# A turn of the context attention with its jobs dealt out anew over four head groups

## The chip, the cores and the metric

The kernel runs on one core of a Trainium2 chip. The metric is the device time of one execution in microseconds (us). The core's engines work side by side, each through its own program in order, and wait for each other on semaphores: PE (TensorE) multiplies and transposes into PSUM, ACT (ScalarE) and DVE (VectorE) drain PSUM and do elementwise work, POOL (GpSimd) works in SBUF, and SP (SyncE) issues loads and stores.

## The reference, cut to what matters

The kernel computes two transformer layers. The change lies in the cross attention of the second one, from 512 rows of each of 8 batches to 77 context rows, with 16 heads of 32 columns:

```python
q = _split_heads(Q @ Wq.T + bq, N_HEAD)
k = _split_heads(K @ Wk.T + bk, N_HEAD)
v = _split_heads(V @ Wv.T + bv, N_HEAD)
score = jnp.einsum('bhqd,bhkd->bhqk', q, k) / jnp.sqrt(jnp.float32(d_k))
attn = jax.nn.softmax(score, axis=-1)
out = jnp.einsum('bhqk,bhkd->bhqd', attn, v)
return out @ Wo.T + bo
...
x = x + jnp.tanh(g_xattn[1]) * _L1_xattn_ref(_layernorm(x, axis=-1), ctx_1024, ctx_1024, ...)
```

Keys and values of the context (k, v) are made long before, in the first pass. What is left here is the normalisation, q, the scores, the softmax, the sum over v, and the projection with Wo.

## The kernel before

The program is a row of passes, with a barrier between two of them. `context_attention_pass` (L1857) is the fifth of seven. It takes a batch of 512 rows in a **turn** `b` (0 to 7), and a turn in four **groups** `c` (0 to 3). Group c does the softmax of four heads at once, the *quad* (b, c). A group has four **slots** j.

Beside this softmax, each turn has sixteen **jobs** for PE. A job fills one of two PSUM banks (`pj_ps`), and another engine drains the bank:

- x0 to x3 (L2090): transposes of the normalised rows (`rows_b`), one of four column blocks each. ACT copies the bank to `xth` rounded (L2169), DVE subtracts to make the rest `xtl` (L2248).
- q0 to q3: products with Wq (`weights_a`), 12 matmuls each, since `split3` (L108) multiplies high and low halves in three terms. ACT drains with the bias (L2175).
- att0 to att3 (L2103): probabilities times values, one for each quad. ACT and DVE drain to `ath` and `atl` (L2178, L2248), as for x.
- out0 to out3: products with Wo (`weights_b`), 12 matmuls each, one for each tile of 128 rows. DVE drains into the residual rows `XR` (L2243).

The jobs are dealt out by hand. `TURN` lists for each group the jobs as (kind, number, lag); lag -1 is a job of the batch before, +1 of the batch after. `SLOT` gives each job its slot. From both comes `SEQUENCE`, the order of all jobs, and from it the bank of each: a job uses the bank of the one two places ahead of it (`former`), and PE waits until that one is drained. `AHEAD` is done before turn 0, `LATE` behind turn 7.

Every engine walks through the same groups and slots (`clock`):

- PE in slot j of group c: the jobs of the slot, then the transposes of head j of the quad before (L2123, into two further banks, "T0" to "T3" below); in slot 1 then also the scores of the next quad (L2114, "S1" in group 0 to "S0" of the next batch in group 3). The scores have one buffer and wait until DVE has subtracted in it.
- DVE: at a group's start the maximum (L2254) and the subtraction (L2257) of the quad's scores, then the drains of slots 0 and 1, then the sums (L2264) and their reciprocal (L2266), then the drains of slots 2 and 3. In slot 3 of group 1 come the statistics of the rows of batch b + 2 (L574 to L584), in slot 3 of group 3 their scaling (L589). In the last two turns there are none; in group 1 of both stands the split of a weight of the next pass (L2282).
- ACT: the exponential (L2198) at slot 1, ahead of the drains of that slot; each head's transposes are copied (L2183), and att needs all four copies of its quad.
- POOL: probabilities times reciprocals (L2063), which T0 waits for; the bias onto the residual rows (L2055) in group 0.
- SP: keys of the next batch behind S1 and S3, values behind att3, the store of a batch and the reload of `XR` behind its out3.

```python
earlier = former(turn, task)
if earlier:
    pe.wait_ge(taken[earlier[0]], earlier[2] * C + earlier[1] + 1)
```

These lines of `job` on PE (L2084 and after) are the wait for the bank.

## Time and profile before

| | us |
|---|---|
| median of 3 runs | 2549.83 |
| lowest and highest | 2549.44, 2553.63 |
| the profiled execution | 2550.44 |
| its span | 2548.7 |
| PE busy | 2326.8 |
| DVE busy | 1390.9 |
| ACT busy | 1060.3 |
| POOL busy | 607.2 |
| context attention, from the first transposes to the last product | 1489.2 to 1884.9 |

A row of the timeline gives the start and the length of an instruction or of a run of equal ones, and in brackets how long its engine was idle before it and who released it. Matmuls overlap: the distance from one start to the next start tells how long PE was kept. A product is twelve rows of L108 at 0.23 us from start to start. The granted clock of TensorE is 1.00 at 2.4 GHz and 0.50 at 1.2 GHz.

### The profile page before, as it was taken

How to read it: one execution, taken by the hardware profiler on the slowest of the kernel's cores; microseconds unless marked ns; L12 is line 12 of the kernel's file. 1: busy time of each engine (PE TensorE's matmuls, PEld its weight loads, DVE VectorE, ACT ScalarE, POOL GpSimd, SP SyncE). 2: the span in 40 equal slices, each digit the busy share in tenths (PEclk: the TensorE clock that was granted, in tenths of full speed). 3: DMA queues.
4: the chain of work that ended last, by engine and by line, in shares of the span. 5: the costliest groups of instructions: out<-in, count | busy, mean ns of one | idle time of the engine just before them, and what ended most of it. 6: DMA issues, size and time to landing. Idle time of an engine off the chain costs nothing. (4 is left out here: it accounts for less than half of the span.)

```text
span 2548.7 us, 40730 instructions
## 1 busy us (share of the span) xinstructions
PE 2326.8 (91%) x16307; PEld 1545.2 (61%) x16348; DVE 1390.9 (55%) x1717; ACT 1060.3 (42%) x1228; POOL 607.2 (24%) x213
## 2 busy tenths in 40 slices
PE   8899999999999987899999779999878999999989
PEld 6655554555555544455555346766656888888867
DVE  7665646556555444777777567677534222222235
ACT  5445445454454442555555544444433222211223
POOL 0045546455464651000000013323210000000000
PEclk9899999999999988999999989999988999999989
DMA  9410101101010103111111221222231000000046
GB/s 299 183 40 12 50 10 48 43 11 47 10 49 11 42 30 113 45 51 50 55 56 34 69 79 58 73 81 77 93 115 55 33 33 33 33 18 32 17 165 215
DMA packets 102014, 163.73 MB, mean 64 GB/s; under 512 B 16996, under 2 KB 39524, under 8 KB 99102
## 3 DMA queue, kind: packets, MB, share of 16 engines
q1 hardware_dynamic: 95918, 150.82, 17.9%
q10 hardware_dynamic: 6000, 11.54, 1.2%
q8 instruction: 71, 1.16, 0.2%
q14 instruction: 25, 0.20, 0.0%
HBM read 112.63 MB, written 49.71 MB: 64 GB/s over the span
## 5 line engine op out<-in xcount | busy, mean ns | idle before, releaser
L1152 DVE TENSOR_REDUCE att_mx<-att_sn 128x2 f32<-128x1024 f32 x196 | 239.8, 1223 | 150.8 <-PE att_sn L961 148.9
L1061 ACT ACTIVATE att_num<-att_st 128x2048 f32<-128x2048 f32 x128 | 240.5, 1879 | 148.2 <-PE att_st L942 89.6
L865 POOL TENSOR_TENSOR att_es<-att_es,att_num 128x2048 f32<-128x2048 f32 x64 | 294.6, 4604 | 15.0 <-ACT att_num L1061 8.7
L861 POOL TENSOR_TENSOR att_es<-att_num 128x2048 f32<-128x2048 f32 x32 | 145.8, 4557 | 366.0 <-PE att_pj L922 341.6
L2541 ACT ACTIVATE rec_ga<-rec_g,rec_bg 128x512 f32<-128x512 f32 x84 | 57.1, 687 | 309.2 <-PE rec_g L2442 309.2
L2442 PE MATMUL rec_g<-weights_a_h,row_weights_h 128*128 128x512 f32 x384 | 153.6, 400 | 14.0 <-ACT rec_ga L2541 11.1
L2442 PE MATMUL rec_g<-weights_a_l,row_weights_h 128*128 128x512 f32 x384 | 152.1, 396 | 0.0
L2442 PE MATMUL rec_g<-weights_a_h,row_weights_l 128*128 128x512 f32 x384 | 151.8, 395 | 0.0
L562 POOL TENSOR_TENSOR ffn_ln_rstd<-ffn_ln_var,ffn_ln_power 128x4 f32<-128x4 f32 x8 | 22.0, 2755 | 464.0 <-DVE ffn_ln_var L584 464.0
L1475 PE MATMUL ffn_h<-ffn_xqt,ffn_w 128*128 128x512 bf16 x486 | 116.3, 382 | 16.3 <-DVE ffn_hs L1736 12.8
L2063 POOL TENSOR_TENSOR xat_pr<-xat_e,xat_rd 128x1232 f32<-128x1232 f32 x32 | 72.9, 2278 | 244.2 <-DVE xat_rd L2266 237.5
L915 PE MATMUL att_pj<-att_num,att_v 128*32 128x512 f32 x1024 | 125.1, 608 | 0.9 <-DVE att_rd L1134 0.9
L1736 DVE TENSOR_TENSOR ffn_hs<-ffn_h,ffn_fb 128x1024 f32<-128x1024 f32 x64 | 78.1, 1220 | 83.1 <-PE ffn_h L1475 83.1
L1488 PE MATMUL ffn_c<-ffn_hs,ffn_dg 32*32 32x512 f32 x3072 | 110.5, 606 | 8.2 <-issue 5.3
L2606 DVE SCALAR_TENSOR_TENSOR rec_ga<-rec_ga,rec_c 128x512 f32<-128x512 f32 x32 | 22.1, 691 | 172.7 <-ACT rec_ga L2541 172.7
L562 POOL TENSOR_TENSOR rec_ln_rstd<-rec_ln_var,rec_ln_power 128x4 f32<-128x4 f32 x7 | 7.5, 1067 | 421.4 <-DVE rec_ln_var L584 421.4
L1624 ACT ACTIVATE ffn_ss<-ffn_c,conv_bias 128x512 f32<-128x512 f32 x128 | 77.4, 692 | 67.2 <-PE ffn_c L1488 61.5
L961 PE MATMUL att_sn<-att_kh,att_qh 32*128 32x512 f32 x392 | 96.5, 487 | 8.9 <-DVE att_mx L1152 8.7
L2183 ACT ACTIVATE xat_pt<-xat_pt 77x512 f32<-77x512 f32 x128 | 73.6, 588 | 74.6 <-PE xat_pt L2123 74.2
L961 PEld LDWEIGHTS att_sn<-att_kh,att_qh 32*128 32x128 f32 x392 | 37.3, 185 | 107.8 <-DVE att_mx L1152 57.0
L1475 PEld LDWEIGHTS ffn_h<-ffn_xqt,ffn_w 128*128 128x128 bf16 x512 | 46.9, 99 | 84.3 <-DVE ffn_hs L1736 19.3
L2123 PEld LDWEIGHTS xat_pt<-xat_ident,xat_pr 128*77 128x77 f32 x512 | 64.9, 157 | 50.1 <-issue 20.8
(407 smaller groups left out, 5800.6 us busy)
## 6 DMA issues: line engine op xcount, KB each, us to landing
rows<-in_x SPq DMA_DIRECT2D x16, 1024.0 KB, 5.4
rows<-x SPq DMA_DIRECT2D x16, 1024.0 KB, 5.2
rows_b<-in_fside_BxSxS SPq DMA_DIRECT2D x8, 1024.0 KB, 7.9
heads<-att_o SPq DMA_DIRECT2D x32, 256.0 KB, 2.3
weights_b_l<-heads SPq DMA_DIRECT2D x8, 1024.0 KB, 5.3
x<-ffn_xr SPq DMA_DIRECT2D x32, 256.0 KB, 2.1
xat_xr<-x SPq DMA_DIRECT2D x8, 1024.0 KB, 5.2
out_x<-x SPq DMA_DIRECT2D x8, 1024.0 KB, 8.8
```

What stands on the lines that cost most here:

```text
L861: pool.tensor_tensor(ES[:], E[0][:], E[1][:], ALU.add).then_inc(s_sum, 1)
L865: pool.tensor_tensor(ES[:], ES[:], E[k][:], ALU.add).then_inc(s_sum, 1)
L915: last = pe.matmul(out[heads(j), :], V[:, k, c * P + DH * j:c * P + DH * j + DH], E[k][:, j, :], start=(k == 0), stop=(k == T - 1))
L961: last = pe.matmul(sn_ps[:, r, :], QT[0][c][own, m // 2 * P:m // 2 * P + P], KT[0][c][own, :], start=True, stop=True)
L1061: act.activation(E[k][:], st_ps[:], ACT.Exp, scale=SCALE).then_inc(s_exp, 1)
L1152: dve.tensor_reduce(MX[c % 2][:, m // 2, 2 * DH * (m % 2):2 * DH * (m % 2) + DH + 1:DH], sn_ps[:], AX, ALU.max, negate=True).then_inc(s_ma ...
L1475: last = pe.matmul(h_ps[:, m, :], W1[:, k, i * P:i * P + P], XQT[:, k, :], start=(k == 0), stop=(k == C - 1))
L1488: last = pe.matmul(c_ps[quarter(m), r, :], DG[quarter(r), 3 * (HG * group + m) + k, :], HS[group % 2][quarter(r), m, k:k + S], start=(k == ...
L1624: act.activation(SS[:, i, :], c_ps[:, r, :], ACT.Silu, bias=CB[:, i:i + 1]).then_inc(s_silu, 1)
L1736: dve.tensor_tensor(HS[group % 2][:, 2 * half:2 * half + 2, 1:S + 1], h_ps[:], FB[:].unsqueeze(1).broadcast_to([P, 2, S]), ALU.mult).then_ ...
L2183: act.activation(PT[d % 2][j][:], pt_ps[j % 2][0:G, :], ACT.Copy).then_inc(s_pte, 1)
L2442: last = pe.matmul(g_ps[m % 2][n][:], W[n][a][:, k, m * P:m * P + P], R[c][:, k, :], start=(part == 0 and k == 0 and i == 0), stop=((part ...
```

## The change

The two tables and the list of jobs ahead of turn 0 are changed, nothing else:

```diff
-    TURN = [[("att", 2, -1), ("q", 3, 0), ("x", 0, 1), ("x", 1, 1), ("x", 2, 1), ("x", 3, 1)],
-            [("att", 3, -1), ("q", 0, 1), ("out", 0, -1), ("out", 1, -1)],
-            [("out", 2, -1), ("out", 3, -1), ("att", 0, 0)],
-            [("att", 1, 0), ("q", 1, 1), ("q", 2, 1)]]
-    SLOT = {("att", 2): 0, ("q", 3): 1, ("x", 0): 2, ("x", 1): 2, ("x", 2): 3, ("x", 3): 3,
-            ("att", 3): 0, ("q", 0): 1, ("out", 0): 2, ("out", 1): 3,
-            ("out", 2): 0, ("out", 3): 1, ("att", 0): 2,
-            ("att", 1): 0, ("q", 1): 1, ("q", 2): 2}
-    AHEAD = [("x", c, 0) for c in range(C)] + [("q", c, 0) for c in range(3)]
+    TURN = [[("q", 2, 0), ("att", 2, -1), ("q", 3, 0)],
+            [("att", 3, -1), ("x", 0, 1), ("x", 1, 1), ("out", 0, -1), ("out", 1, -1)],
+            [("out", 2, -1), ("x", 2, 1), ("x", 3, 1), ("out", 3, -1), ("att", 0, 0)],
+            [("q", 0, 1), ("att", 1, 0), ("q", 1, 1)]]
+    SLOT = {("q", 2): 0, ("att", 2): 1, ("q", 3): 2,
+            ("att", 3): 0, ("x", 0): 1, ("x", 1): 1, ("out", 0): 2, ("out", 1): 3,
+            ("out", 2): 0, ("x", 2): 1, ("x", 3): 1, ("out", 3): 2, ("att", 0): 3,
+            ("q", 0): 0, ("att", 1): 1, ("q", 1): 2}
+    AHEAD = [("x", c, 0) for c in range(C)] + [("q", c, 0) for c in range(2)]
```

On PE a turn reads, before and after, with the transposes of heads (T) and scores (S) in their places:

| group | before | after |
|---|---|---|
| 0 | att2 T0 q3 T1 S1 x0 x1 T2 x2 x3 T3 | q2 T0 att2 T1 S1 q3 T2 T3 |
| 1 | att3 T0 q0 T1 S2 out0 T2 out1 T3 | att3 T0 x0 x1 T1 S2 out0 T2 out1 T3 |
| 2 | out2 T0 out3 T1 S3 att0 T2 T3 | out2 T0 x2 x3 T1 S3 out3 T2 att0 T3 |
| 3 | att1 T0 q1 T1 S0 q2 T2 T3 | q0 T0 att1 T1 S0 q1 T2 T3 |

The first place is the step from group 1 to group 2 on DVE, in the loop over the middle turns. `rows` and `xat_ln` belong to the statistics, `xat_mx` and `xat_sm` to the scores, `xat_xr` is the drain of out, `xat_xtl` that of x. Before:

```order
L580 MEMSET xat_ln_var 128x4
L582 BN_AGGR xat_ln_mv<-xat_ln_stats 128x2 x4
L52 REGISTER_ALU
L584 TENSOR_REDUCE xat_ln_var<-xat_ln_mv 128x4
L2253 REGISTER_ALU
L2254 TENSOR_REDUCE xat_mx<-xat_s 128x16
L2257 TENSOR_TENSOR xat_sm<-xat_s,xat_mx 128x1232
L2243 SCALAR_TENSOR_TENSOR xat_xr<-xat_pj,xat_tg,xat_xr 128x512 x2
L2264 TENSOR_REDUCE xat_su<-xat_e 128x16
```

The same place after:

```order
L580 MEMSET xat_ln_var 128x4
L582 BN_AGGR xat_ln_mv<-xat_ln_stats 128x2 x4
L52 REGISTER_ALU
L584 TENSOR_REDUCE xat_ln_var<-xat_ln_mv 128x4
L2253 REGISTER_ALU
L2254 TENSOR_REDUCE xat_mx<-xat_s 128x16
L2257 TENSOR_TENSOR xat_sm<-xat_s,xat_mx 128x1232
L2243 SCALAR_TENSOR_TENSOR xat_xr<-xat_pj,xat_tg,xat_xr 128x512
L2247 REGISTER_ALU
L2248 TENSOR_TENSOR xat_xtl<-xat_pj,xat_xth 128x512
```

Out2's drain is where it was, behind the statistics, the maximum and the subtraction; out3's has moved behind the drains of x2 and x3 and the sums.

The second place is group 2 on PE in turn 6, written out without the loop. There the last matmuls of out2 were followed by T0 and out3:

```order
L108 MATMUL xat_pj<-weights_b_h,xat_atl 128x512
L2123 MATMUL xat_pt<-xat_ident,xat_pr 77x128 x4
L108 MATMUL xat_pj<-weights_b_h,xat_ath 128x512
L108 MATMUL xat_pj<-weights_b_l,xat_ath 128x512
L108 MATMUL xat_pj<-weights_b_h,xat_atl 128x512
```

After the change:

```order
L108 MATMUL xat_pj<-weights_b_h,xat_atl 128x512
L2123 MATMUL xat_pt<-xat_ident,xat_pr 77x128 x4
L2090 MATMUL xat_pj<-xat_ident,rows_b 128x128 x8
L2123 MATMUL xat_pt<-xat_ident,xat_pr 77x128 x4
L2114 MATMUL xat_s<-xat_k,xat_qt 128x77 x16
L108 MATMUL xat_pj<-weights_b_h,xat_ath 128x512
```

The transposes x2 and x3 (L2090, eight matmuls), a transpose of heads and the scores S3 stand between out2 and out3.

## Rows read from the trace of the kernel before

**Rows 1.** The page's first part: busy time of the engines.

```profile
PE 2326.8 (91%) x16307; PEld 1545.2 (61%) x16348; DVE 1390.9 (55%) x1717; ACT 1060.3 (42%) x1228; POOL 607.2 (24%) x213
```

**Rows 2.** Windows: start:end, length, busy time per engine, PEclk, DMA share, GB/s.

```profile
1489.20:1549.20 60.00, 49.99 (x348) 36.45 (x348) 38.91 (x56) 23.29 (x35) 12.68 (x8) 0.77 0.27 81
1549.20:1816.90 267.70, 246.15 (x2021) 186.53 (x2017) 188.34 (x237) 126.10 (x194) 86.74 (x35) 1.00 0.25 82
1816.90:1885.80 68.90, 54.31 (x328) 38.52 (x324) 36.89 (x46) 22.30 (x33) 18.93 (x7) 0.80 0.18 60
```

**Rows 3.** Timeline of PE, a middle turn: start, length, instruction, [idle before <- releaser].

```profile
1642.92 1.09 PE L2090 MATMUL xat_pj<-xat_ident,rows_b 128*128 128x128 f32 x8
1643.85 0.60 PE L2123 MATMUL xat_pt<-xat_ident,xat_pr 128*77 128x128 f32 x4
1644.99 1.25 PE L2090 MATMUL xat_pj<-xat_ident,rows_b 128*128 128x128 f32 x8 [0.54 <-DVE xat_xtl L2248]
1647.45 1.06 PE L2103 MATMUL xat_pj<-xat_pt,xat_v 77*32 77x512 f32 x8 [0.78 <-DVE xat_xtl L2248]
...
1659.44 0.60 PE L2123 MATMUL xat_pt<-xat_ident,xat_pr 128*77 128x128 f32 x4
1659.79 0.48 PE L108 MATMUL xat_pj<-weights_b_h,xat_ath 128*128 128x512 f32 x1
...
1662.67 0.60 PE L2123 MATMUL xat_pt<-xat_ident,xat_pr 128*77 128x128 f32 x4
...
1670.31 1.06 PE L2103 MATMUL xat_pj<-xat_pt,xat_v 77*32 77x512 f32 x8 [0.73 <-ACT xat_pt L2183]
1671.80 0.66 PE L2123 MATMUL xat_pt<-xat_ident,xat_pr 128*77 128x128 f32 x4 [0.42 <-POOL xat_pr L2063]
...
1681.49 1.06 PE L2103 MATMUL xat_pj<-xat_pt,xat_v 77*32 77x512 f32 x8 [0.95 <-ACT xat_pt L2183]
...
1686.28 1.13 PE L2114 MATMUL xat_s<-xat_k,xat_qt 32*128 32x77 f32 x32
1687.34 1.09 PE L2090 MATMUL xat_pj<-xat_ident,rows_b 128*128 128x128 f32 x8
```

**Rows 4.** Timeline of DVE in the same turn.

```profile
1659.63 0.75 DVE L2243 SCALAR_TENSOR_TENSOR xat_xr<-xat_pj,xat_tg,xat_xr 128x512 f32<-128x512 f32 x1 [2.49 <-PE xat_pj L108]
1660.30 2.46 DVE L574 BATCH_NORM_STATS2 xat_ln_stats<-rows 128x6 f32<-128x512 f32 x4
...
1663.32 1.44 DVE L2254 TENSOR_REDUCE xat_mx<-xat_s 128x16 f32<-128x1232 f32 x1
...
1666.15 1.40 DVE L2243 SCALAR_TENSOR_TENSOR xat_xr<-xat_pj,xat_tg,xat_xr 128x512 f32<-128x512 f32 x2
...
1675.91 3.85 DVE L589 TENSOR_SCALAR rows_b<-rows,xat_ln_mv,xat_ln_rstd 128x512 f32<-128x512 f32 x4
```

**Rows 5.** Timeline of PE: three of its idle stretches over 2 us.

```profile
88.39 1.97 PE L885 MATMUL att_st<-ident,rows 128*128 128x128 f32 x8 [3.71 <-ACTq L1012]
...
1822.90 1.13 PE L2114 MATMUL xat_s<-xat_k,xat_qt 32*128 32x77 f32 x32 [2.14 <-DVE xat_sm L2257]
...
2436.67 0.77 PE L108 MATMUL rec_pj<-row_weights_h,rec_ch 128*128 128x512 f32 x1 [7.17 <-DVE row_weights_l L2375]
```

**Rows 6.** Windows of two falls of the clock, behind waits of 2.67 and 2.14 us.

```profile
899.40:902.80 3.40, 3.40 (x26) 1.53 (x18) 1.38 (x2) 0.60 (x1) 0.00 (x0) 0.50 0.00 0
1824.40:1834.60 10.20, 9.06 (x60) 5.91 (x58) 6.45 (x7) 4.54 (x8) 7.75 (x3) 0.50 0.39 119
```

**Rows 7.** Timeline of PE at half clock: scores, a product, the transposes behind it.

```profile
1830.78 2.01 PE L2114 MATMUL xat_s<-xat_k,xat_qt 32*128 32x77 f32 x32
1832.71 0.79 PE L108 MATMUL xat_pj<-weights_b_h,xat_ath 128*128 128x512 f32 x1
...
1836.48 0.60 PE L2123 MATMUL xat_pt<-xat_ident,xat_pr 128*77 128x128 f32 x4
```

**Rows 8.** Timeline of PE, turn 7: the scores behind out3.

```profile
1848.05 1.13 PE L2114 MATMUL xat_s<-xat_k,xat_qt 32*128 32x77 f32 x32 [1.27 <-DVE xat_sm L2257]
```

## The prediction, written before the changed kernel had run

> **What bounds the kernel now.** TensorE is busy for 91% of the span [rows 1], so I look first for the places where it stands idle inside the edited pass, and then for what it would wait on in the new order. The pass takes 396.6 us. Its middle, turns 1 to 6, is 267.7 us long and TensorE works in 246.2 us of it at a granted clock of 1.00 (2.4 GHz); the start and the end of the pass have lower shares and a lower mean clock, 0.77 and 0.80 [rows 2]. The middle repeats itself exactly: the first two transposes of rows start at 1642.92 us and again at 1687.34 us, so a turn is 44.42 us [rows 3]. In it PE stands idle five times, for 0.54 us (x2 waits until VectorE has drained x0), 0.78 (att3 waits for x1's drain), 0.73 (att1 waits for the copies of its transposes), 0.42 (the transposes wait for POOL's probabilities) and 0.95 us (att2 waits for copies) [rows 3]. That is 3.42 us in a turn. More than that times seven, 24 us or 0.9% of the kernel, no new order can win in this pass.
>
> VectorE is the other engine to watch. It is in order: what stands behind the moments in its program waits for them. In [rows 4] it drains out1 at 1659.63, takes the four statistics from 1660.30, then the maximum and the subtraction of group 2 from 1663.32 on, and only then drains out2, from 1666.15 on. Now this costs PE nothing: behind out2 come out3, two transposes and the scores, and nothing asks for out2's bank before att0.
>
> **The change, part by part.** No instruction is added or taken away: 16 jobs in a turn, each with the same shape. What changes is what stands between two jobs of the same bank, since a job waits until the job two places ahead of it is drained.
>
> *Waits that go.* Now there are two products in every group. x2 and x3 no longer follow x0 and x1 directly: 0.54 and some 0.18 us inside the second pair go. att3 no longer follows x3: 0.78 goes. att1 now has q0 and a transpose ahead of it, so its copies and POOL's probabilities are in time: 0.73 and 0.42 go. The 0.95 us stay: "product, two transposes, att" is still there, now ahead of att3 in place of att2. Together 2.65 us less in a turn.
>
> *The wait that comes: x3 on out2's drain.* The new sequence is out0, out1, out2, x2, x3, out3. x3 uses out2's bank and comes after one product, one transpose and x2. Counted from the transposes behind out1 (1659.44 in the old trace): 0.35 to out2, 2.88 for it, 0.60 for transposes that no product follows, 0.47 for x2 make 4.30 us until PE wants x3 [rows 3]. VectorE's work between out1 and out2 is the same as before (the order above): out2's drain starts 6.71 us after those transposes (1666.15), takes 0.75, and PE starts some 0.15 later: 7.6 us [rows 4]. So x3 waits 7.6 - 4.30 = **3.3 us** in each of turns 1 to 5. In turn 6, as in turn 7, a weight split stands in place of the moments, and the subtraction ends later: S3, which PE would want 7.1 us behind those transposes (two products of 2.88, three transposes of 0.35, 0.35 and 0.60), waits 1.27 us for it there [rows 8]; with the drain of 0.75 that makes 7.1 + 1.27 + 0.75 - 4.30, some 4.8 us. Everything behind x3 on PE (transposes, S3, out3, att0) is held up with it, and POOL and ScalarE only follow.
>
> *Smaller waits that come.* S1 is now in group 0, after two products, but group 0's maximum and subtraction come behind the scaling of the rows (3.85 us [rows 4]), and the chain to them starts at att0, which has moved a slot later. Between nothing and the 2.14 us that S1 waits for the same subtraction in the last turn [rows 5]; I take 0.6, nearer to nothing, since two products, five transposes and att2 (some 8.7 us) lie between S0 and S1, and the scaling, the maximum and the subtraction behind it come to about 7, only starting late. x1 now waits for att3's drain and out0 for x0's: each between 0 and the 0.78 us of the wait of this kind in [rows 3]; I take 0.4 and 0.2. With 0.2 for two transposes fewer that a product follows, a steady turn gets 3.3 + 0.6 + 0.4 + 0.2 + 0.2 - 2.65 = **2.05 us longer**.
>
> *Sum without the clock.* Turns 1 to 6: 6 x 2.05 = 12.3, and 1.5 more for turn 6. Turn 0 has no out products to hide behind; q2 now comes later and fills one of its waits: between 0 and -4, I take -2. In turn 7 out3 no longer stands ahead of S3, which waits for VectorE anyway (1.27 us [rows 8]), but behind it and ahead of att0, from which the closing chain runs: out3 and its transposes, 3.2 us, and 0.8 for a longer wait of S1: +4. That makes **+16 us**.
>
> *The clock.* This is the larger unknown. I listed all idle stretches of PE of over 2 us that began at full clock: 14 in the whole trace; the first ends at 88.39, the shortest, of 2.14 us, at 1822.90, the last at 2436.67 [rows 5]. After every one of them the granted clock was 0.50 (1.2 GHz) for a stretch, of 3.4 us the shortest, 10.2 us for the one behind the 2.14 us [rows 6]. In turns 1 to 6 there is no such wait so far, and the clock is 1.00 throughout. A wait of 3.3 us is of this kind, so I expect a fall in each of turns 1 to 6. What is then slower: scores take 1.93 us in place of 1.06, and a product in whose course the clock comes back 3.77 in place of 2.88 [rows 3, 7]; with x3 and a transpose (1.0 us, doubled) that is 0.87 + 0.89 + 0.97 = **2.7 us** for one fall, 16 us for six. Bounds: 0, and 5.1 us (10.2 us at half clock, PE working all through).
>
> The Trainium skill, "TensorE: Matmul & The Clock Gate", section "HAM oscillation — how this bites in real kernels", puts the penalty at half of the throttled time, paid anew at every long gap of a loop. By this page and the 10.2 us of [rows 6] it would be 31 us for six falls and the sum +47. This trace has falls of 3.4 us too [rows 6], and for those the same rule gives 1.7 us each.
>
> Sum: 16 + 16 = **+32 us**. The profiled execution took 2550.44 us, of which 2548.7 are the span; the median of the three runs is 2549.83, 0.6 us less. I go from the median: 2582 us.
>
> **Nothing else.** The loads are not nearer to their use: keys, values and the reload of the residual rows follow S1, att3, S3 and the last out, and the residual rows are needed some 10 us after they land. The passes behind this one start after a barrier and only shift.
>
> **The rivals.**
> 1. *Forecast*: new wait of x3, and the clock falls behind it. +32, own range +24 to +40. For it: 14 of 14. Chance 0.67; falls in some turns only lie between this and the next, in the range of either.
> 2. *The wait comes, the clock stays up.* PE has worked densely until x3, and short transposes surround the wait; its length could spare it. +16: 2566. Chance 0.15.
> 3. *Long falls.* A fall lasts 10.2 us every time, PE working in all of it: 6 x 5.1 = 31, +47: 2597. For it: the fall behind the shortest of the 14 waits was that long; against it: others last 3.4 us, and out3 and q0 are dense work [rows 6]. Chance 0.08. It is the price that the page named above gives.
> 4. *No change.* x3 waits 1.3 us only, because the statistics are finished ahead of out1's end, and the gains of 2.65 cancel the small waits. Against it: they stand behind out1's drain in VectorE's program. 0.03.
> 5. *Faster.* The mechanism is the one the even split suggests: out2's drain comes early enough, x3 doesn't wait. Then a turn gets 3.3 - 2.05 = 1.25 us shorter, 7.5 us over six, 2 in turn 0, less 4 in turn 7: -5.5, 2544. It decides at a wait of 3.3 - 2.05 = 1.25 us for x3: below it a turn is shorter, above it longer. This needs VectorE to drain out2 some 2 us sooner than [rows 4] shows, with the same instructions ahead. Chance 0.07, with errors in my reading of the order.
>
> **How the numbers follow.** A measurement of this kernel can tell 0.2%, 5 us. Predicted is the forecast, 2582. The range of 2564 to 2592 holds the forecast's own and rival 2; left out are rivals 3 to 5, 0.18. Slower 0.90 (the first three), same 0.03, faster 0.07.
>
> **What would show it.** In the table of waits a new line, PE x transposes waiting for VectorE's drain of the output (L2090 on L2243), six times, some 21 us; the lines for PE waiting for the row drains (xtl) and for POOL shrink in the middle of the pass. A turn of 48 to 50 us in place of 44.4, or 46.5 if the clock holds. In the windows of the turns a granted clock under 1.00. Wrong would be: a turn under 44.4; no such line; or falls of the clock without a longer turn. VectorE's, ScalarE's and POOL's busy times stay as they are; PE's grows by what runs at half clock.

## The result and the profile after

The changed kernel takes 2573.39 us (median of 4 runs, 2570.99 to 2577.69) against 2550.05 us (4 runs, 2549.44 to 2553.63): the ratio is 1.0093, with an interval of 1.0077 to 1.0109. It is 23.3 us slower. The forecast was 2582 us, the range 2564 to 2592. The profiled execution took 2574.59 us, 2572.8 of which are the span.

The page's busy times after the change, which answer to [rows 1]:

```profile
PE 2340.6 (91%) x16348; PEld 1554.2 (60%) x16348; DVE 1390.9 (54%) x1717; ACT 1055.8 (41%) x1228; POOL 607.4 (24%) x213
```

VectorE's and POOL's times are the same within 0.2 us, ScalarE's is 4.5 us shorter, for which no cause was looked for. PE is busy for 13.8 us more, though it has the same work. 5.3 us of them lie ahead of the pass, where nothing was changed (1347.2 and 1352.4 us) and where the trace of before lacks the 41 matmul records by which 16307 and 16348 differ. Inside the pass it is 11.5 us more, since some of the work now runs at a lower clock, and behind it 2.9 less.

Windows of the kernel after, for the start, the middle and the end of the pass, cut like [rows 2] at T0 of group 0 in turns 1 and 7 (start:end, length, busy us and instructions of PE, PEld, DVE, ACT and POOL, granted clock, DMA share, GB/s):

```profile
1489.80:1546.90 57.10, 47.72 (x341) 36.95 (x342) 36.33 (x55) 21.94 (x34) 12.80 (x8) 0.78 0.25 69
1546.90:1837.10 290.20, 259.44 (x2018) 196.24 (x2016) 190.21 (x239) 122.96 (x194) 86.74 (x35) 0.95 0.24 79
1837.10:1912.40 75.30, 54.81 (x333) 40.08 (x331) 36.22 (x45) 22.15 (x34) 18.93 (x7) 0.82 0.16 55
```

The pass, from its first transposes to its last product, grew from 395.7 to 422.7 us, by 27.0. The middle accounts for most of it: 267.7 us at a granted clock of 1.00 became 290.2 us at 0.95, +22.5. The start is 2.9 us shorter. The end is 7.3 us longer (its last product ended at 1884.9 before, and ends at 1912.4 now). Of both, 1.0 us is only where the cut stands: att2 comes ahead of T0 before and behind it after, so for the same work the start is 1.9 us shorter and the end 6.3 us longer. Outside the pass the program is 0.6 us longer ahead of it and 3.4 us shorter behind it (660.4 us against 663.8). Together that is +24.1 in the span.

The new line in the table of waits after the change (engine and line, released by; us in total, times, the longest), with the two that grew, for the whole pass:

```profile
PE xat_pj L2090 <- DVE xat_xr L2243: 20.9, 6, 4.6
PE xat_s L2114 <- DVE xat_sm L2257: 9.6, 10, 4.1
PE xat_pt L2123 <- POOL xat_pr L2063: 9.5, 3, 3.3
```

The first line is the wait that the prediction named, six times and 20.9 us. The scores waited 6.5 us, 5 times, in the pass before, and the transposes of heads 8.1 us, 10 times, for POOL; these 10 are now 3, two in the first turn and one in the last.

PE's timeline of the kernel after, in a middle turn, answers to [rows 3] (start, length, instruction, [idle before <- releaser]):

```profile
1654.45 0.66 PE L2090 MATMUL xat_pj<-xat_ident,rows_b 128*128 128x128 f32 x4 [0.40 <-DVE xat_atl L2248]
...
1665.98 0.60 PE L2123 MATMUL xat_pt<-xat_ident,xat_pr 128*77 128x128 f32 x4
1666.42 0.60 PE L2090 MATMUL xat_pj<-xat_ident,rows_b 128*128 128x128 f32 x4
1670.26 0.66 PE L2090 MATMUL xat_pj<-xat_ident,rows_b 128*128 128x128 f32 x4 [3.25 <-DVE xat_xr L2243]
1670.76 0.60 PE L2123 MATMUL xat_pt<-xat_ident,xat_pr 128*77 128x128 f32 x4
1671.29 1.49 PE L2114 MATMUL xat_s<-xat_k,xat_qt 32*128 32x77 f32 x32
1672.71 0.79 PE L108 MATMUL xat_pj<-weights_b_h,xat_ath 128*128 128x512 f32 x1
...
1676.78 0.60 PE L2123 MATMUL xat_pt<-xat_ident,xat_pr 128*77 128x128 f32 x4
```

x2 (1666.42) has its bank, x3 (1670.26) has not, and idles for 3.25 us. VectorE's timeline of the kernel after shows why; it answers to [rows 4]:

```profile
1662.95 0.75 DVE L2243 SCALAR_TENSOR_TENSOR xat_xr<-xat_pj,xat_tg,xat_xr 128x512 f32<-128x512 f32 x1 [2.48 <-PE xat_pj L108]
1663.62 2.46 DVE L574 BATCH_NORM_STATS2 xat_ln_stats<-rows 128x6 f32<-128x512 f32 x4
...
1666.63 1.44 DVE L2254 TENSOR_REDUCE xat_mx<-xat_s 128x16 f32<-128x1232 f32 x1
1668.11 1.44 DVE L2257 TENSOR_TENSOR xat_sm<-xat_s,xat_mx 128x1232 f32<-128x1232 f32 x1
1669.47 0.74 DVE L2243 SCALAR_TENSOR_TENSOR xat_xr<-xat_pj,xat_tg,xat_xr 128x512 f32<-128x512 f32 x1
```

The drain of out1 starts at 1662.95 and the drain of out2 at 1669.47, 6.52 us apart, as in [rows 4] (1659.63 and 1666.15). The order on VectorE and its durations are the old ones. What changed is only that PE now asks for out2's bank early.

Behind the wait the clock falls. A window of the kernel after, 1.6 us behind x3's start:

```profile
1671.90:1675.30 3.40, 3.40 (x26) 2.78 (x23) 2.32 (x4) 0.36 (x1) 0.88 (x1) 0.50 0.12 23
```

There is one such fall with each of the six waits, 3.4 us long in turns 2 to 5 and 6.8 us in turns 1 and 6. In turn 1 it begins 0.8 us before the wait ends, in the others behind it. From x3 to the next transposes of heads (1670.26 to 1676.78) PE needs 6.52 us. At full clock the same four pieces (0.50 for x3, 0.53 for a transpose, 1.06 for the scores, 2.88 for a product) make 4.97. So a fall of 3.4 us costs 1.55 us here. A turn is 47.67 us long (the rows' first transposes start at 1653.44 and again at 1701.11); it was 44.42.

### The profile page after: what moved, and what is told of

Its sections match the earlier page's. It is cut to its first block and busy times, and to the rows that moved or that the text cites. A ratio compares the mean times of both kernels' runs of the same rounds, so it can differ in the third digit from the quotient of the medians.

```text
span 2572.8 us, 40766 instructions
## 1 busy us (share of the span) xinstructions
PE 2340.6 (91%) x16348; PEld 1554.2 (60%) x16348; DVE 1390.9 (54%) x1717; ACT 1055.8 (41%) x1228; POOL 607.4 (24%) x213
## 5 line engine op out<-in xcount | busy, mean ns | idle before, releaser
L1475 PE MATMUL ffn_h<-ffn_xqt,ffn_w 128*128 128x512 bf16 x512 | 123.8, 385 | 12.8 <-DVE ffn_hs L1736 12.8
L1475 PEld LDWEIGHTS ffn_h<-ffn_xqt,ffn_w 128*128 128x128 bf16 x512 | 47.2, 99 | 85.4 <-issue 20.9
```

The lines of the kernel that those rows point to most:

```text
L1475: last = pe.matmul(h_ps[:, m, :], W1[:, k, i * P:i * P + P], XQT[:, k, :], start=(k == 0), stop=(k == C - 1))
```

## The experiments

Every kernel was timed beside the kernel before on the same chip. "Before" in a ratio is that one, with medians of 2548.1 to 2549.0 us. A kernel derived from "the changed kernel" keeps its tables except where the diff says otherwise.

### 1. The changed kernel, its statistics taken elsewhere

The statistics of group 1 (3.0 us of VectorE's work with what is computed from them, 1663.62 to 1666.63 above) move one slot earlier, from behind out1's drain to ahead of it. PE's program is left as it is.

```diff
-                    if not last and j == 3 and c in (1, 3):
-                        normalise(b + 2, c // 2)
+                    if not last and (c, j) in ((1, 2), (3, 3)):
+                        normalise(b + 2, ((1, 2), (3, 3)).index((c, j)))
```

> The changed kernel with the row statistics of VectorE moved one slot earlier in group 1: from behind the drain of out1 to between the drains of out0 and out1, so that they run beside PE's product out1. Theory A (x3 waits 3.25 us because statistics, maximum and subtraction stand between the drains of out1 and out2): 3.06 us leave that stretch, x3's wait falls to under 0.6 us, the turn from 47.7 to about 44.2 us, no fall of the clock in turns 1 to 5, and the whole to about 2552 us (2546 to 2557), turn 6 keeping its long wait since a weight split stands there. Theory B (VectorE has simply too much to do in group 1, 11 us of work): the wait only moves, to out0's or out1's bank or to S3, and the whole stays at 2568 or more.

Measured: 2550.16 us (10 runs), ratio 1.0001, interval 0.9992 to 1.0011. VectorE's timeline of this kernel has the statistics between out0's and out1's drains now, and only the maximum and the subtraction between those of out1 (1606.44) and out2 (1609.93):

```profile
1603.42 2.46 DVE L574 BATCH_NORM_STATS2 xat_ln_stats<-rows 128x6 f32<-128x512 f32 x4
...
1606.44 0.75 DVE L2243 SCALAR_TENSOR_TENSOR xat_xr<-xat_pj,xat_tg,xat_xr 128x512 f32<-128x512 f32 x1
1607.11 1.43 DVE L2254 TENSOR_REDUCE xat_mx<-xat_s 128x16 f32<-128x1232 f32 x1
1608.57 1.44 DVE L2257 TENSOR_TENSOR xat_sm<-xat_s,xat_mx 128x1232 f32<-128x1232 f32 x1
1609.93 0.74 DVE L2243 SCALAR_TENSOR_TENSOR xat_xr<-xat_pj,xat_tg,xat_xr 128x512 f32<-128x512 f32 x1
```

PE's timeline has the wait of x3 at 0.66 us:

```profile
1610.72 0.66 PE L2090 MATMUL xat_pj<-xat_ident,rows_b 128*128 128x128 f32 x4 [0.66 <-DVE xat_xr L2243]
```

The line of waits of this kernel, for the pass:

```profile
PE xat_pj L2090 <- DVE xat_xr L2243: 7.9, 6, 4.6
```

A turn takes 43.57 us and the clock doesn't fall in turns 1 to 5. Of the six waits five are short; turn 6 keeps its 4.63 us and its fall, since there the weight split stands in that place and not the statistics. This is the decisive run: with PE's order untouched, moving 3 us of another engine's work removes the whole slowdown (1.0093 to 1.0001). With the statistics there a middle turn is 0.85 us shorter than in the kernel before (0.37 us shorter than in experiment 4, where the old tables have the statistics in the same place). This is lost again in turn 6, which is some 5 us longer than before, and at the end of the pass, where the waits of 3.12, 4.06 and 6.07 us described below remain.

### 2. The wait filled with work, the clock held

Ahead of x3 PE makes 26 transposes into a bank that is free there. Nobody reads them; the wait stays, only PE isn't idle in it.

```diff
+                if kind == "x" and i == 3 and not (isinstance(turn, int) and turn == -1):
+                    pe.wait_ge(s_pte, turn * H + HG)
+                    for _ in range(26):
+                        pe.transpose(pt_ps[1][:, 0:P], ident[:], ident[:])
```

> The changed kernel with 26 transposes of the identity into a free bank ahead of x3's wait (some 3.0 us of PE work that nobody reads), so that the wait stays as long but PE is not idle in it. If the falls of the clock behind that wait cost what the trace says (1.5 us where they last 3.4 us, 2.8 us in turn 1), the turns 2 to 5 go from 47.66 to 46.1 us, and the whole is 8 to 12 us shorter, near 2563. Theory of no cost (PE would catch up elsewhere in the turn, since S1 waits for VectorE anyway): the same 2573 within 3 us. If idle alone, not its depth, decided, the clock would still fall.

Measured: 2564.53 us (4 runs), ratio 1.0055, interval 1.0039 to 1.0072. PE's timeline of this kernel, where the wait was, and two windows: five of its turns, and its whole middle, cut as above:

```profile
1661.72 3.00 PE L2088 MATMUL xat_pt<-xat_ident 128*128 128x128 f32 x26
1665.13 0.66 PE L2094 MATMUL xat_pj<-xat_ident,rows_b 128*128 128x128 f32 x4 [0.41 <-DVE xat_xr L2247]
```

```profile
1556.00:1786.70 230.70, 220.54 (x1813) 169.90 (x1812) 162.43 (x210) 99.42 (x161) 73.53 (x31) 1.00 0.22 72
1545.97:1824.34 278.37, 264.60 (x2174) 203.83 (x2172) 190.08 (x239) 122.85 (x194) 86.81 (x35) 1.00 0.25 82
```

x3 starts as late as ever, but the clock is 1.00 over five whole turns, and a turn takes 46.15 us. By the ratios (1.0093 against 1.0055) the clock's part of the slowdown is 0.0038 of 2550 us, about 9.7 us; by the medians it is 8.9. What is left, 14 to 16 us, is the wait itself and the longer end. A turn of the loop shows the split: 44.42 without the wait, 46.15 with it, 47.67 with a fall of 3.4 us, so 1.73 for the order of work and 1.52 for the clock, near the 1.55 us read from the timeline. Counted from T0 of group 0 to the next, turn 1 is 49.03 us against 46.32, turns 2 to 5 are 1.50 to 1.54 us apart, and turn 6 is 50.51 against 47.45. So the six falls cost 2.7, four times 1.5, and 3.1 us: 11.8 us, which is also the difference of the two middles (290.2 and 278.4). In the total 8.9 of them arrive. The two traces differ by 1 to 2.5 us each at the start of the pass, ahead of it and behind it too.

### 3. x2 and x3 behind out3

The two transposes of rows get one more product's time before they ask for their banks.

```diff
-            [("out", 2, -1), ("x", 2, 1), ("x", 3, 1), ("out", 3, -1), ("att", 0, 0)],
+            [("out", 2, -1), ("out", 3, -1), ("x", 2, 1), ("x", 3, 1), ("att", 0, 0)],
```

> The changed kernel with x2 and x3 behind out3 (slot 2 of group 2) in place of ahead of it. Theory A: out3 is then the cover for out2's drain, and x3 waits for out3's drain instead, which VectorE does behind the sums; S3 stands ahead of out3 and waits for the subtraction some 2.7 us. So the wait moves from x3 to S3 and the turn stays within 0.5 us of what it is (47.2 to 47.7 us), the whole at 2568 to 2574. If only the place of x3 mattered: the turn falls by 3 us or more, the whole to 2553 or less.

Measured: 2574.44 us (4 runs), ratio 1.0092, interval 1.0075 to 1.0109: the same as the changed kernel. It is 0.4 us over the expected range. x3 waits 0.48 us, and this line of waits has grown (it was 9.6 us):

```profile
PE xat_s L2113 <- DVE xat_sm L2256: 30.9, 16, 4.1
```

The scores S3 now wait 2.68 us in each of turns 1 to 5 for the subtraction of group 2, which stands behind the same statistics, and behind each of these waits the clock falls for 3.4 us too. In turn 6, behind the weight split, they wait 4.06 us and the fall lasts 6.8 us. A turn is 47.63 us. PE must not want anything of VectorE's between out1's drain and out2's earlier than VectorE gets there; which of PE's steps asks is unimportant.

### 4. The kernel before, its statistics moved in the same way

The statistics' new place without the new tables: the diff is that of experiment 1, on the kernel before.

> The kernel before with the same move of the statistics, from slot 3 to slot 2 of group 1. It tells how much of a1's gain belongs to the statistics in any order. Nothing waits for VectorE behind out1 there, except in the last two turns; replayed with the trace's durations, POOL's probabilities of group 2 come earlier, and the turn falls by 0.6 us: 2546 us (2543 to 2550), a gain of 0.1 to 0.2%. If the gain is as large as a1's (over 10 us), theory A's reading, that the new order created the stretch, is wrong.

Measured: 2547.61 us (10 runs), ratio 0.9994, interval 0.9984 to 1.0004. A turn takes 43.94 us in place of 44.42. In the old order the move takes 0.48 us off a turn, too little for the total to show clear of noise; in the new one it is worth 24 us. So experiment 1 didn't find a general gain of that size that happens to cancel a loss. With the statistics in this place both tables are alike: 1.0001 and 0.9994, their intervals overlapping.

### 5. The queries' move alone

The half of the change that touches q and out: x0 to x3 stay in group 0. (The diffs here and in experiment 6 are against the kernel before. Here and in experiments 3, 6 and 10 the slots and the jobs ahead of turn 0 follow the table; the diff shows the table alone.)

```diff
-    TURN = [[("att", 2, -1), ("q", 3, 0), ("x", 0, 1), ("x", 1, 1), ("x", 2, 1), ("x", 3, 1)],
-            [("att", 3, -1), ("q", 0, 1), ("out", 0, -1), ("out", 1, -1)],
+    TURN = [[("q", 2, 0), ("att", 2, -1), ("q", 3, 0), ("x", 0, 1), ("x", 1, 1), ("x", 2, 1), ("x", 3, 1)],
+            [("att", 3, -1), ("out", 0, -1), ("out", 1, -1)],
...
-            [("att", 1, 0), ("q", 1, 1), ("q", 2, 1)]]
+            [("q", 0, 1), ("att", 1, 0), ("q", 1, 1)]]
```

> One part of the change alone: the products are dealt out as in the changed kernel (q2, q3 in group 0, q0, q1 in group 3, two products in every group), the four transposes of rows stay together in group 0 as before. Theory A: x3 no longer waits for out2. But group 1 then holds no q between att3 and out0, so PE comes to out1 and S3 sooner and VectorE's statistics, maximum and subtraction end last all the same: S3, in slot 1 of group 2 with only out2 ahead of it, waits some 2.7 us, S2 some 1 us, a turn takes 47 us without falls of the clock, and the whole 2570 to 2580, as slow as the full change. Rival: the rows' transposes are what costs, and without their move the even deal of products pays: a turn under 44.4 us and the whole under 2550.

Measured: 2583.96 us (4 runs), ratio 1.0144, interval 1.0127 to 1.0161: 4 us over what was expected. The waits came as expected (S3 2.68 us, S2 1.02 us), but not the clock: it falls in every one of turns 1 to 6. PE's timeline and the table of waits of this kernel:

```profile
1625.59 2.00 PE L2113 MATMUL xat_s<-xat_k,xat_qt 32*128 32x77 f32 x32 [2.68 <-DVE xat_sm L2256]
```

```profile
PE xat_s L2113 <- DVE xat_sm L2256: 39.4, 23, 4.1
```

With q0 gone from group 1, S3 comes too early for the subtraction of group 2, as in experiment 3. The turns alternate between some 48.5 and 50 us, as the falls behind the waits do between 3.4 and 6.8 us. This half of the change is worse than the whole: in the changed kernel x0 to x3 stand in the time that q0's leaving opens ahead of S3, and S3 doesn't wait there in turns 1 to 6.

### 6. The rows' transposes alone

The other half: x0 and x1 in group 1, x2 and x3 in group 2; q2 stays in group 3.

```diff
-    TURN = [[("att", 2, -1), ("q", 3, 0), ("x", 0, 1), ("x", 1, 1), ("x", 2, 1), ("x", 3, 1)],
-            [("att", 3, -1), ("q", 0, 1), ("out", 0, -1), ("out", 1, -1)],
-            [("out", 2, -1), ("out", 3, -1), ("att", 0, 0)],
-            [("att", 1, 0), ("q", 1, 1), ("q", 2, 1)]]
+    TURN = [[("att", 2, -1), ("q", 3, 0)],
+            [("att", 3, -1), ("x", 0, 1), ("x", 1, 1), ("out", 0, -1), ("out", 1, -1)],
+            [("out", 2, -1), ("x", 2, 1), ("x", 3, 1), ("out", 3, -1), ("att", 0, 0)],
+            [("q", 0, 1), ("att", 1, 0), ("q", 1, 1), ("q", 2, 1)]]
```

> The other part alone: rows' transposes two and two behind att3 and out2, out3 behind S3 and q0 in group 3 as in the changed kernel, q2 still ahead of the batch's turn (three products in group 3, one in group 0). Theory A: the stretch from out1 to x3 is the same, x3 waits 3.25 us for out2's drain, the clock falls behind it, a turn takes some 48 us, the whole 2570 to 2580. Rival: the wait needs q2's move too: a turn under 46 us.

Measured: 2587.46 us (4 runs), ratio 1.0156, interval 1.0139 to 1.0173: 7 us over what was expected. PE's timeline, the table of waits and a window behind one of the waits:

```profile
1672.49 0.66 PE L2089 MATMUL xat_pj<-xat_ident,rows_b 128*128 128x128 f32 x4 [3.25 <-DVE xat_xr L2242]
```

```profile
PE xat_pj L2089 <- DVE xat_xr L2242: 20.9, 6, 4.6
```

```profile
1673.60:1680.40 6.80, 6.80 (x44) 5.60 (x45) 2.84 (x4) 0.89 (x2) 3.23 (x2) 0.50 0.06 12
```

The wait is that of the changed kernel to the hundredth, in each turn and in total. The pass is 434.3 us long, 11.7 more than in the changed kernel. From turn 1's rows to turn 7's it is 6.8 us (1558.04 to 1804.25, against 1556.92 to 1796.37). Its falls in turns 1 to 6 last 6.8, 3.4, 6.8, 6.8, 6.8 and 10.2 us, where the changed kernel has 6.8, 3.4 four times and 6.8; the one turn with a fall of 3.4 us is the shortest, 48.10 us against 49.30 to 49.66. What goes with the length is when the fall begins: in both kernels those that begin 1.4 us or more behind x3's start last 3.4 us, and those that begin earlier, from 2.1 us ahead of that start to 1.1 us behind it, last 6.8 or 10.2. Why the moment differs from kernel to kernel and from turn to turn wasn't settled.

### 7. A table made for VectorE's order

If the reason is that PE asks VectorE for something too early, then a table whose jobs ask late enough should beat both kernels. Of PE's jobs and VectorE's instructions with the durations and waits of these traces I worked out a table in which the jobs of a middle turn should hardly wait; its statistics stand in slot 1 of group 2.

```diff
+    TURN = [[("q", 1, 0), ("att", 2, -1), ("q", 2, 0), ("q", 3, 0)],
+            [("x", 0, 1), ("att", 3, -1), ("x", 1, 1), ("x", 2, 1), ("out", 0, -1), ("x", 3, 1)],
+            [("out", 1, -1), ("out", 2, -1), ("q", 0, 1)],
+            [("out", 3, -1), ("att", 0, 0), ("att", 1, 0)]]
+    SLOT = {("q", 1): 0, ("att", 2): 0, ("q", 2): 1, ("q", 3): 3, ("x", 0): 0, ("att", 3): 1,
+            ("x", 1): 1, ("x", 2): 3, ("out", 0): 3, ("x", 3): 3, ("out", 1): 0, ("out", 2): 1,
+            ("q", 0): 3, ("out", 3): 0, ("att", 0): 0, ("att", 1): 2}
+    AHEAD = [("x", c, 0) for c in range(C)] + [("q", c, 0) for c in range(1)]
...
+                    if not last and (c, j) in ((2, 1), (3, 3)):
+                        normalise(b + 2, ((2, 1), (3, 3)).index((c, j)))
```

> A table of its own, found by replaying the waits with the trace's durations: q1, q2, q3 in group 0, the rows' transposes singly between other jobs (x0, x1, x2, x3 in slots 0, 1, 3, 3 of group 1, each with a job of another kind between), out0 to out3 from the end of group 1 on, q0 at the end of group 2, att0 and att1 in group 3, and the statistics in slot 1 of group 2, behind the drain of out2. Every drain then has a product or several jobs to hide behind. Expected: a turn of 40.8 us, no idle of PE over 1 us in it and no fall of the clock, the pass 40 us shorter than before, the whole at 2508 us (2500 to 2518). If VectorE's chain through the softmax and not the order of the drains bounded the turn, it would stay over 43 us and the whole over 2535.

Measured: 2515.21 us (4 runs), ratio 0.9869, interval 0.9852 to 0.9885. One turn and all of the middle of this kernel, as windows:

```profile
1627.70:1668.50 40.80, 40.63 (x338) 30.84 (x337) 31.93 (x43) 19.93 (x33) 14.45 (x7) 1.00 0.26 85
1545.00:1790.00 245.00, 242.76 (x2012) 184.16 (x2011) 188.23 (x239) 123.20 (x194) 84.85 (x35) 1.00 0.27 89
```

A turn is 40.83 us, and PE is busy in 40.63 of the 40.80 us shown; the same 16 jobs took 44.42 and 47.67. The total lies in the expected range. The pass is 360.0 us long, 35.7 less than before, where 40 were expected. By PE's busy time hardly anything is left in the middle for another order. The prediction's bound was 3.42 us in a turn, its waits; 44.42 - 40.83 is 3.59, all of it and 0.17 more.

### 8. Experiment 1 with the weights' split two groups later

If turn 6's 4.63 us come from the weight split in its group 1, they go when the split does. All three splits of the next pass's weights come two groups later, on ScalarE and VectorE:

```diff
-                at = (b - B + 2) * C + c if isinstance(b, int) else -1
+                at = (b - B + 2) * C + c - 2 if isinstance(b, int) else -1
```

> a1 (statistics in slot 2) with the three splits of the next pass's weights in the last two turns two groups later, so that turn 6 has none in group 1. Theory A holds for the end as for the middle: turn 6's wait of x3 (4.63 us) is the split standing between the drains of out1 and out2, so it goes to under 1.5 us, and the whole is 4 to 9 us shorter than a1 (2550.2), near 2543. If that wait came from something else in turn 6, nothing changes.

Measured: 2548.13 us (10 runs), ratio 1.0000, interval 0.9990 to 1.0009. PE's timeline of this kernel at x3 in turn 6:

```profile
1787.07 0.66 PE L2090 MATMUL xat_pj<-xat_ident,rows_b 128*128 128x128 f32 x4 [0.29 <-DVE xat_xr L2243]
```

The wait is gone as expected (0.29 for 4.63), and the pass is 390.9 us, 6.1 less than in experiment 1: the middle is 7.3 us shorter and the end 1.1 us longer, where a split now stands (the last product waits 4.78 us for VectorE in place of 3.06). But the profiled spans are alike (2546.9 and 2547.0 us), and so are the ratios. The pass begins 2.5 us later in this trace, and the part behind it is 3.4 us longer (663.8 and 660.4 us). There, with the same instructions, the clock is at 0.50 for 34.8 us in this trace and for 27.2 in experiment 1's. This expectation wasn't borne out for the total: a gain of 6 us inside the pass didn't arrive at the end of the program.

### 9. Experiment 7 with the statistics at their old place

Which part of experiment 7's gain is the table's and which the statistics' is told by leaving them at the end of group 1:

```diff
-                    if not last and (c, j) in ((2, 1), (3, 3)):
-                        normalise(b + 2, ((2, 1), (3, 3)).index((c, j)))
+                    if not last and j == 3 and c in (1, 3):
+                        normalise(b + 2, c // 2)
```

> best1's table of jobs with the statistics where they were, in slot 3 of group 1. It tells the table's share of best1's gain from the statistics' share. In this table out0 is drained ahead of x3 in that slot and the statistics stand behind both; out1 comes in group 2. By theory A the statistics then delay only the maximum and subtraction of group 2 and out1's drain, which out2, T1 and S3 cover: a turn of 41.1 us (best1: 40.83), the whole at 2517 us, 0 to 7 us more than best1. If the statistics' place were what made best1 fast, it would be over 2530.

Measured: 2520.06 us (4 runs), ratio 0.9880, interval 0.9861 to 0.9899. A turn is 41.11 us, as expected. By the ratios the statistics' new place is worth 0.0011, 3 us, with intervals that overlap: a table whose jobs don't ask between out1's and out2's drains hardly minds where the statistics are. The table is the gain.

### 10. A second table, with the late split

Another table of the same kind, with statistics in the last slot of group 2 and the split of experiment 8, to see how much depends on the one table.

```diff
+    TURN = [[("q", 1, 0), ("att", 2, -1), ("q", 2, 0), ("q", 3, 0)],
+            [("x", 0, 1), ("att", 3, -1), ("x", 1, 1)],
+            [("out", 0, -1), ("out", 1, -1), ("x", 2, 1), ("x", 3, 1), ("out", 2, -1), ("q", 0, 1)],
+            [("out", 3, -1), ("att", 0, 0), ("att", 1, 0)]]
```

> A second table found in the same way, with out0 and out1 both in slot 0 of group 2, x2 and x3 behind them, statistics in slot 3 of group 2, and the weight splits two groups later. By replay a turn of 40.7 us and an end some 3 us shorter than best1's: 2511 us (2505 to 2518), that is no measurable difference or a small gain over best1's 2515. PE is then busy for all but 0.5 us of a turn, so a turn well under 40.6 us would speak against the reading that PE bounds it.

Measured: 2514.53 us (4 runs), ratio 0.9858, interval 0.9838 to 0.9878: not to be told from experiment 7. A turn is 40.67 us, as expected; the shorter end isn't there (the pass is 361.6 us, 1.6 more than in experiment 7). One turn of this kernel as a window:

```profile
1587.90:1628.50 40.60, 40.53 (x338) 30.87 (x336) 32.03 (x43) 19.55 (x33) 14.46 (x7) 1.00 0.25 85
```

## Why the prediction was right, and where it was not

The total, 2573.39 us, lies in the range, which was drawn around rivals 1 and 2 together. Measured from the median it started from, +23.6, it is just short of the forecast's own +24 to +40: mechanism and places came as said, the sum was a good third too high.

**The wait that comes** was right in place, cause and size: forecast 3.3 us in turns 1 to 5 and some 4.8 in turn 6, measured 3.25 and 4.63, 20.9 us in all against "some 21". Experiment 1 shows the cause: take the statistics out from between the two drains, and the wait is 0.66.

**That the clock falls behind it** was right (six waits, six falls), and experiment 2 shows that it falls because PE idles. **Its price** is the term that was mis-sized: 2.7 us for one fall and 16 us for six were forecast. The falls of 3.4 us cost 1.5 each, those of 6.8 us 2.7 and 3.1, all six 11.8 (experiment 2). The 2.7 us were worked out for a fall that begins together with x3. In turns 2 to 5 it begins 1.5 to 1.9 us behind x3's start, at 1671.9 in the rows above. I had let x3 and the transpose behind it run at half clock too (0.97); from 1670.26 to 1671.29 they take 1.03 us, as at full clock. The scores I had wholly at half clock (0.87 more); to the product's start they take 1.42 in place of 1.06, 0.36 more. The product, for which [rows 7] gave 0.89 more, took 1.19 (4.07 for 2.88, 1672.71 to 1676.78). 0.36 + 1.19 is the 1.55: the step that failed is the one that let every fall begin together with x3. The rule of the Trainium skill ("TensorE: Matmul & The Clock Gate", section "HAM oscillation — how this bites in real kernels"), half of the throttled time, gives 1.7 us for a fall of 3.4 us and 3.4 for one of 6.8. The traces, 1.5 and 2.7 to 3.1, lie somewhat below both. The price of the long falls (10.2 us each, rival 3) didn't come: none of the six was longer than 6.8 us.

**The small terms of a turn.** S1 waits 0.23 us where 0.6 was taken; x1 0.40, as taken; out0 some 0.1 where 0.2 was taken. The turn without the clock was forecast at 44.42 + 2.05 = 46.47 us and is 46.15 in experiment 2. The 1.5 us more for turn 6 were counted wrongly. The forecast added x3's longer wait, but turn 6 of the kernel before already waits for the same weight split, at S3, and that wait goes. PE's timeline of the kernel before, turn 6:

```profile
1800.98 1.13 PE L2114 MATMUL xat_s<-xat_k,xat_qt 32*128 32x77 f32 x32 [1.27 <-DVE xat_sm L2257]
```

So turn 6 without the clock is 1.8 us longer (45.61 to 47.45), where 2.05 + 1.5 = 3.55 were forecast. Turns 1 to 6 together: forecast 12.3 + 1.5 + 16, some +30; measured +22.5, of which 10.7 are the order and 11.8 the clock.

**The start** gave 1.9 us on the same work where I took 2 from between 0 and 4. That is luck in part: the q2 term was an estimate without rows, and the clock is low there in both traces (0.77 and 0.78), so what is the order and what the clock wasn't told apart. **The end** was forecast at +4 and is +6.3 on the same work. PE's timeline of the kernel after, turn 7 and what follows; the fence answers to [rows 5] and [rows 8]:

```profile
1842.41 1.90 PE L2114 MATMUL xat_s<-xat_k,xat_qt 32*128 32x77 f32 x32 [3.12 <-DVE xat_sm L2257]
...
1868.97 1.22 PE L2114 MATMUL xat_s<-xat_k,xat_qt 32*128 32x77 f32 x32 [4.06 <-DVE xat_sm L2257]
...
1885.53 1.14 PE L2123 MATMUL xat_pt<-xat_ident,xat_pr 128*77 128x128 f32 x4 [6.07 <-ACT xat_pt L2183]
1889.73 3.81 PE L2123 MATMUL xat_pt<-xat_ident,xat_pr 128*77 128x128 f32 x16 [3.06 <-POOL xat_pr L2063]
...
1898.49 0.77 PE L108 MATMUL xat_pj<-weights_b_h,xat_ath 128*128 128x512 f32 x1 [2.98 <-DVE xat_atl L2248]
```

The last three of these in the kernel before:

```profile
1859.17 1.14 PE L2123 MATMUL xat_pt<-xat_ident,xat_pr 128*77 128x128 f32 x4 [3.86 <-ACT xat_pt L2183]
1862.77 3.81 PE L2123 MATMUL xat_pt<-xat_ident,xat_pr 128*77 128x128 f32 x16 [2.46 <-POOL xat_pr L2063]
...
1871.68 0.77 PE L108 MATMUL xat_pj<-weights_b_h,xat_ath 128*128 128x512 f32 x1 [1.53 <-DVE xat_atl L2248]
```

S1 waits 3.12 in place of 2.14, 1.0 more where I had 0.8. S3 waits 4.06 in place of 1.27: out3 is no longer ahead of it, which I had said, and had priced as out3 and its transposes (3.2 us) behind it. What I left out are the waits that come after, in the closing chain: 6.07 in place of 3.86, 3.06 in place of 2.46 and 2.98 in place of 1.53 us. That they grew because less of PE's work is left to stand in them is the likely reason, not one that a run shows.

**Behind the pass** I had written "only shift". It became 3.4 us shorter, with the same instructions: the clock is at 0.50 there for 27.1 us, and was for 34.8 before. That lies outside anything I had a term for. Summed, on the same work: start -1.9, middle +22.5, end +6.3, ahead +0.6, behind -3.4 make +24.1 in the span; the medians differ by 23.3. The forecast of +32 was 8.7 too high against these 23.3. The middle makes +7.5 of that (30 for 22.5; some 4.4 of them are the clock, 1.7 turn 6, the rest the small terms), the part behind the pass +3.4 and the difference of medians and spans +0.8; the end makes -2.3, the part ahead -0.6 and the start -0.1. So errors of both signs stand in the sum.

**The bound** of 24 us, which "no new order can win in this pass", was wrong. It was worked out from the waits of a middle turn, and the tables of experiments 7 and 10 made the pass 35.7 and 34.1 us shorter. 21.6 us of experiment 7's gain lie in the middle. The other 14 lie in the start and the end, where PE was idle for 10 and some 14 us by [rows 2], which the bound had left out. The forecast doesn't rest on it.

**The signs.** The new line of waits came, six times and 20.9 us. The turn came out at 47.67 us, just under the "48 to 50" that was written down, for the reason given for the price.

**The rivals.** Rival 2 (the clock stays up, +16) isn't what happened, but it is what experiment 2 made, at 1.0055, +14. Rival 4 (statistics finished ahead of out1's end) fell: the statistics start at 1663.62, behind out1's drain. Rival 5 (no wait of x3, -5.5) names the point that decides, x3's wait of 1.25 us. Experiment 1 lies below it, at 0.66, and its turn is indeed shorter, 43.57 (also than the 43.94 of experiment 4, so that this isn't the statistics' place alone). Its total isn't faster, because of turn 6 and the end. Those two terms would have to be taken away too, and in experiment 8 one of them was, with no gain in the total.

**What stays open.** How the time outside the pass answers to a shift of a few us (experiment 8); and what sets the moment at which a fall begins, with which its length goes (experiment 6).

## What to carry to other kernels

Before moving jobs of one engine, write down what the other engine does in order between two drains of the same ring of buffers, and count from the last common event when the mover will ask and when the drain can come: here that gave 3.3 us for 3.25. If a gap can't be closed by the mover's order, look at the other engine's order too: in the changed kernel, moving 3 us of its work that nobody waits for just then was worth 24 us, and a table that heeds its order is 33 to 34 us faster than the kernel before. An even split of work over groups says nothing about when it is asked for; and where TensorE's wait can't be avoided, filling it can keep the clock up, which was worth 9 us here, a good third of the damage.

## What the runs showed of the hardware

- Idles of PE of 2.1 us and more were mostly followed by a fall of the granted clock from 1.00 to 0.50 (2.4 to 1.2 GHz): 14 of 14 in the kernel before, and every wait of 2.68 us in experiment 3. In the traces of all twelve kernels it was 200 of 211 (of those that began at full clock, without the one ahead of the first matmul). The eleven others, from 2.20 to 3.72 us long, lie in nine kernels. One is in experiment 2: PE's timeline of that kernel, and the windows of the idle and of what follows it:

```profile
1515.74 0.66 PE L2127 MATMUL xat_pt<-xat_ident,xat_pr 128*77 128x128 f32 x4 [3.14 <-POOL xat_pr L2063]
```

```profile
1512.50:1515.80 3.30, 0.16 (x2) 0.06 (x1) 3.23 (x4) 0.69 (x1) 2.25 (x1) 1.00 0.00 0
1515.80:1519.20 3.40, 3.40 (x52) 3.10 (x52) 0.79 (x2) 2.76 (x5) 0.00 (x0) 1.00 0.00 0
```

  Another is the idle of 3.7 us of which [rows 5] has the end at 88.39. In the kernel before a fall comes with it, as in nine of the twelve kernels; in experiments 1, 6 and 9 none does, though up to there the programs are the same. The windows of the idle and of what follows it in experiment 1:

```profile
84.30:88.00 3.70, 0.01 (x1) 0.01 (x1) 0.00 (x0) 1.30 (x3) 0.08 (x2) 1.00 0.45 189
88.00:91.40 3.40, 3.20 (x25) 2.61 (x25) 2.00 (x4) 2.62 (x5) 2.04 (x10) 1.00 1.08 454
```

  So the length of an idle alone doesn't decide; 14 of 14 was a good rule for this forecast, not a law. There are falls without such an idle as well: one of 10.2 us begins at 121.1 in the kernel before, where PE's longest idle nearby is 1.62 us.
- The same wait, in the same place of the loop, brought falls of different lengths (3.4 and 6.8 us in the changed kernel, mostly 6.8 in experiment 6). A fall of 3.4 us cost 1.5 us, those of 6.8 us 2.7 and 3.1 (experiment 2).
- The same instructions took 660.4 us behind the pass in one trace and 663.8 in another, with the clock at 0.50 for 27.2 and 34.8 us of them (experiments 1 and 8).
- Transposes whose result is read by nobody hold the clock as well as useful work does: 1.00 over 230.7 us in experiment 2, with a wait of 3 us in each turn.
